# Layer normalisation and router as one block, ranking by the eight largest values, statistics and first expert weights moved ahead

## The reference

```python
x = x + s * g                       # end of layer 0; s is the mixer, g the gate
xn = _layernorm(x, axis=-1)         # (x - mean) / sqrt(var + 1e-5)
s = _L1_attn_ref(xn, ...)
g = _silu(_L1_ffn_ref(xn, ...))     # begins with the router, below
x = x + s * g

router_logits = x @ gate_w.T                            # 16 experts
routing_probs = jax.nn.softmax(router_logits, axis=-1)
topk_w, topk_idx = jax.lax.top_k(routing_probs, K)      # K = 4; of equal values the first wins
topk_w = topk_w / topk_w.sum(axis=-1, keepdims=True)
combine = (jax.nn.one_hot(topk_idx, E) * topk_w[..., None]).sum(1)
shared = _silu_mul(x @ shared_gate_up.T, SI) @ shared_down.T
shared = shared * jax.nn.sigmoid(x @ shared_gate_vec.T)
# then sum over experts of (silu-gated x @ w_gu) @ w_d * combine
```

## Time and profile before

| | |
|---|---|
| median of 3 runs | 2531.27 us (2529.53 to 2531.35) |
| the profiled execution | 2531.68 us |
| its span in the profile | 2530.0 us |
| busy in the span | PE 89%, DVE 73%, ACT 57%, POOL 51% |
| end of the mixer to the first expert matmul | 1518.78 to 1597.53, 78.75 us |

### The profile page before, as it was taken

The page is one execution under the profiler, slowest core; times in us unless marked ns, Lnnn a source line. Parts: engine busy times, 40 slices in busy tenths (PEclk is TensorE's granted clock), DMA queues, the critical chain, the costliest instruction groups (busy, mean ns, idle before and its releaser), DMA issues. The chain is left out here.

```text
span 2530.0 us, 45593 instructions
## 1 busy us (share of the span) xinstructions
PE 2259.8 (89%) x16164; PEld 1793.2 (71%) x16164; DVE 1836.3 (73%) x3256; ACT 1435.5 (57%) x2461; POOL 1289.7 (51%) x1275
## 2 busy tenths in 40 slices
PE   4996999999999999999999972799999995799992
PEld 2785788888888888888888862688888884444432
DVE  5875777777777777777777746677777776777755
ACT  1333778877878787877878851122222224266661
POOL 3451676777767777676876770354554540000000
PEclk9997999999999999999999995899999998799996
DMA  2002112112121121211211220100000002122214
GB/s 90 1 22 111 44 53 74 53 45 90 45 80 47 45 91 45 82 45 53 82 53 57 75 67 1 36 28 21 28 21 28 27 8 96 59 76 81 76 60 137
DMA packets 93441, 141.19 MB, mean 56 GB/s; under 512 B 23713, under 2 KB 62977, under 8 KB 91969
## 3 DMA queue, kind: packets, MB, share of 16 engines
q1 hardware_dynamic: 91200, 133.96, 16.1%
q10 hardware_dynamic: 2048, 4.72, 0.6%
HBM read 118.12 MB, written 20.32 MB: 55 GB/s over the span
## 5 line engine op out<-in xcount | busy, mean ns | idle before, releaser
L1081 DVE SCALAR_TENSOR_TENSOR mix_cv<-mix_pp,mix_cw,mix_cv 128x384 f32<-128x384 f32 (+4 forms) x864 | 490.8, 571 | 215.0 <-ACT mix_cv L999 194.2
L1220 POOL TENSOR_TENSOR ffn_hl<-ffn_h,ffn_hh 128x512 fp32r<-128x512 f32 x112 | 144.9, 1293 | 250.8 <-ACT ffn_hh L1278 250.8
L1024 ACT ACTIVATE mix_lm<-mix_pd 128x512 f32<-128x512 f32 x256 | 153.3, 599 | 205.1 <-PE mix_pd L915 203.1
L851 POOL TENSOR_TENSOR mix_ce<-mix_ce,mix_cv 128x1024 f32<-128x1024 f32 x112 | 266.8, 2382 | 0.0
L75 PE MATMUL mix_pp<-l0in_XH,mix_w_lo 128*128 128x384 f32 (+2 forms) x576 | 243.6, 423 | 22.9 <-DVE mix_w_lo L1069 16.2
L981 PE MATMUL mix_px<-mix_wo,mix_z 128*128 128x256 f32 x1024 | 256.4, 394 | 0.0
L1707 DVE TENSOR_REDUCE att_tops<-att_psc 128x1 f32<-128x512 f32 (+3 forms) x384 | 189.9, 550 | 55.5 <-PE att_psc L1655 32.2
L857 POOL TENSOR_TENSOR mix_zt<-mix_zsq 128x256 f32<-128x256 f32 x128 | 94.2, 736 | 243.0 <-ACT mix_zsq L1032 243.0
L1731 ACT ACTIVATE att_pr<-att_pst 128x1024 f32<-128x1024 f32 (+7 forms) x256 | 156.5, 657 | 103.5 <-PE att_pst L1672 73.5
L1278 ACT ACTIVATE ffn_hh<-ffn_h 128x512 fp32r<-128x512 f32 x112 | 71.1, 635 | 249.0 <-DVE ffn_h L1301 249.0
L981 PEld LDWEIGHTS mix_px<-mix_wo,mix_z 128*128 128x128 f32 x1024 | 186.8, 192 | 20.6
(11 more groups left out here) (332 smaller groups left out, 6873.2 us busy)
## 6 DMA issues: line engine op xcount, KB each, us to landing
mix_ce<-ecs SPq DMA_DIRECT2D x112, 512.0 KB, 3.7
mix_w_raw<-in_w_in SPq DMA_DIRECT2D x8, 1280.0 KB, 5.6
a_part<-att_sums SPq DMA_DIRECT2D x32, 256.0 KB, 5.1
ffn_raw<-in_wgu SPq DMA_DIRECT2D x56, 128.0 KB, 2.2
mix_ll<-cs SPq DMA_DIRECT2D x384, 4.0 KB
mix_wo<-in_w_out SPq DMA_DIRECT2D x8, 512.0 KB, 6.6
ffn_draw<-in_wd SPq DMA_DIRECT2D x28, 128.0 KB, 2.1
q<-qkv_part SPq DMA_DIRECT2D x24, 128.0 KB, 1.9
```

The costliest lines, as they stand in the source:

```text
L851: pool.tensor_tensor(ce[o][:, :, :], ce[o][:, :, :], cv[:, CT_C, cols_of(c)].unsqueeze(1).to_broadcast([P, GH, Q]), ALU.mult).then_inc(ce_ ...
L1024: act.activation(lm[o][:, 4 * i:4 * i + 4, :].rearrange("p h l -> p (h l)"), pd[:, :], ACT.Exp).then_inc(l_done, 1)
L1081: last = dve.scalar_tensor_tensor(out, of, cw[:, g, ct, 3 - d:4 - d], out, ALU.mult, ALU.add)
```

## The change

`layernorm` and `router` become one block, `norm_route`. What it does otherwise:

- The mixer takes bn_stats of each finished row tile at the end of the slot after it (L1022 of the new file), on DVE, behind a wait for `joined`; there is one slot more.
- POOL's pow is made in four parts of four tiles. DVE normalises the even tiles, ACT the odd ones (Identity with scale and shift). Rings are three deep, a unit is two tiles, and PE's router matmuls of a unit follow its turning at once, on 32 padded columns instead of 128; turned logits of all 16 tiles go into one PSUM bank and are copied once.
- The ranking takes the eight largest of each 16 values (MAX), compares with the fourth of them, and settles ties by a running count made with four shifted additions.
- ACT makes Tanh ahead of Exp. ACT makes high parts of the first two tiles of expert weights, POOL low parts, and POOL clears the sum; SP loads these weights at the block's start (`GluWeights`). One half of the last copy to `CW3` moves to ACT.

The diff, cut to its core (the removed `layernorm` and the removed parts of `router` are told above):

```diff
@@ mixer
-        SLOTS = range(-5, NC + 2)
+        SLOTS = range(-5, NC + 3)
...
+                    if LAST <= c - 3 < NC:
+                        i = c - 3 - LAST
+                        dve.wait_ge(joined, i + 1)
+                        dve.bn_stats(stat[:, i, :], ACC[:, i, :])
@@ glu
-                load(0, 0)
-                load(0, 1)
...
-                cut_tile(0, 0)
-                cut_tile(0, 1)
...
-                dve.memset(OUT[:, :, :], 0.0).then_inc(zeroed, 1)
-                dve.wait_ge(zeroed, 1)
@@ norm_route
+                sp.dma_start(w[:, :, 0:NE], w_route).then_inc(w_in, 16)
+                for a in range(2):
+                    weights.load(sp, 0, a, wgu, wd, sel)
...
+                for i in range(4):
+                    t = slice(i * NT // 4, (i + 1) * NT // 4)
+                    pool.tensor_tensor(rstd[:, t], var[:, t], half[:, t], ALU.pow).then_inc(powered, 1)
...
+                pool.wait_ge(logits, 1)
+                for a in range(2):
+                    pool.wait_ge(hi_cut, 3 * a + 3)
+                    pool.tensor_tensor(weights.wl[a][:, :, :, :], weights.raw[a][:, :, :, :],
+                                       weights.wh[a][:, :, :, :].bitcast(F32), ALU.subtract).then_inc(weights.cut, 1)
+                    pool.tensor_tensor(weights.dl[a][:, :], weights.draw[a][:, :], weights.dh[a][:, :].bitcast(F32),
+                                       ALU.subtract).then_inc(weights.split[a], 1)
+                pool.memset(OUT[:, :, :], 0.0).then_inc(cleared, 1)
...
+                for n in range(RING):
+                    turn(n)
+                pe.wait_ge(w_split, 2)
+                for n in range(NU):
+                    project(n)
+                    if n + RING < NU:
+                        turn(n + RING)
+                    if n >= 2 and n % 2 == 0:
+                        turn_logits(n // 2 - 1)
+                turn_logits(NU // 2 - 1)
...
+                act.wait_ge(logits, 1)
+                act.activation(cw[:, :, E:NE], lg[:, :, E:NE], ACT.Tanh, scale=0.5).then_inc(tanhed, 1)
+                act.wait_ge(routed, 2)
+                act.activation(cw[:, :, 0:E], cw[:, :, 0:E], ACT.Exp).then_inc(exped, 1)
+                for a in range(2):
+                    act.wait_ge(weights.w_in[a], 64)
+                    act.activation(weights.wh[a][:, :, :, :], weights.raw[a][:, :, :, :], ACT.Copy).then_inc(hi_cut, 1)
...
+                shift_of(0)
+                normalise(0)
+                normalise(1)
+                shift_of(1)
+                normalise(2)
...
+                for n in range(NU):
+                    low(n)
+                    if n + RING < NU:
+                        normalise(n + RING)
...
+                for t in range(NT):
+                    last = dve.max(top[:, t, :], cw[:, t, 0:E])
+                then(last)
+                least = top[:, :, TOPK - 1:TOPK].to_broadcast([P, NT, E])
...
+                for j, d in enumerate((1, 2, 4, 8)):
+                    to = 1 + j % 2
+                    then(dve.tensor_tensor(tie[to][:, :, PAD:], tie[of][:, :, PAD:], tie[of][:, :, PAD - d:PAD + E - d], ALU.add))
+                    of = to
```

More of the change, by code:

```diff
@@ L1344, in _ @@
[L1344 to L1347 removed]
+                pool.memset(half[:, :], -0.5).then_inc(powered, 1)
+                pool.memset(w[:, :, :], 0.0).then_inc(w_zero, 1)
+                pool.wait_ge(powered, 1)
+                pool.wait_ge(stats, 7)
@@ L1366, in _, with turn @@
-                pe.wait_ge(v, 25)
+                def turn(n):
+                    pe.wait_ge(even, n + 1)
+                    pe.wait_ge(odd, n + 1)
+                    if n >= RING:
+                        pe.wait_ge(lo_done, n - RING + 1)
+                    for j in range(2):
+                        for k in range(KD):
+                            last = pe.transpose(xt[n % RING][:, k * 256 + j * P:k * 256 + (j + 1) * P],
+                                                xn[(2 * n + j) % (2 * RING)][:, k * P:(k + 1) * P], ident[:, :])
+                    last.then_inc(turned, 1)
@@ L1380, in _, with normalise, keep_logits @@
-                act.activation(cw[:, :, E:NE], lg[:, :, E:NE], ACT.Tanh, scale=0.5).then_inc(a, 1)
+                def normalise(n):
+                    t = 2 * n + 1
+                    act.activation(xn[t % (2 * RING)][:, :], X[:, t, :], ACT.Identity, bias=shift[:, t:t + 1],
+                                   scale=rstd[:, t:t + 1]).then_inc(odd, 1)
+                def keep_logits(b):
+                    act.wait_ge(lg_mm, 2 * b + 2)
+                    act.activation(lg_t[:, b * TB:(b + 1) * TB], pl_[b % 2][0:W, :], ACT.Copy).then_inc(lg_kept, 1)
@@ new lines, in _ @@
+                for n in range(RING):
+                    act.wait_ge(shifted, (2 * n + 1) // 4 + 1)
+                    normalise(n)
+                for n in range(NU):
+                    act.wait_ge(turned, n + 1)
+                    act.activation(both(n)[0], turned_of(n), ACT.Copy).then_inc(hi_done, 1)
+                    if n + RING < NU:
+                        act.wait_ge(shifted, (2 * (n + RING) + 1) // 4 + 1)
+                        normalise(n + RING)
+                    if n >= 2 and n % 2 == 0:
+                        keep_logits(n // 2 - 1)
@@ L1412, in _ @@
-                then(dve.tensor_tensor(above[:, :, :, :], above[:, :, :, :], same[:, :, :, :], ALU.add))
-                then(dve.tensor_reduce(rank[:, :, :], above[:, :, :, :], AX.X, ALU.add))
-                then(dve.tensor_scalar(rank[:, :, :], rank[:, :, :], TOPK - 0.5, None, ALU.is_lt))
-                then(dve.tensor_tensor(e, e, rank[:, :, :], ALU.mult))
+                dve.wait_ge(exped, 1)
+                for t in range(NT):
+                    last = dve.max(top[:, t, :], cw[:, t, 0:E])
@@ L1416, in _ @@
+                then(dve.tensor_tensor(order[:, :, :], tie[of][:, :, PAD:], above[:, :].unsqueeze(2).to_broadcast([P, NT, E]), ALU.add))
+                then(dve.scalar_tensor_tensor(keep[:, :, :], order[:, :, :], TOPK + 0.5, tie[0][:, :, PAD:], ALU.is_lt, ALU.mult))
+                then(dve.tensor_tensor(keep[:, :, :], keep[:, :, :], over[:, :, :], ALU.add))
+                then(dve.tensor_tensor(e, e, keep[:, :, :], ALU.mult))
                 then(dve.tensor_reduce(tot[:, :], e, AX.X, ALU.add))
```

302 lines of the change are left out of this document (125 added, 177 removed).

## The result

The changed kernel takes **2488.07 us** (median of 4 runs, 2486.38 to 2495.33) against 2530.4 for the kernel before beside it: a ratio of 0.9841, interval 0.9829 to 0.9853, 42.3 us less. The forecast was 2494 and 36.9 us less, the range 2487 to 2503. A second set of runs gave 0.985 (0.9835 to 0.9865), 38.8 us less.

The account below looks back on a forecast made before the run. The prediction took a 78.75 us chain of waits between the mixer's last row and the first expert matmul as the bound. Gains 4.9 + 11.5 + 13.0 + 7.5 = 36.9 us gave 2494 us, range 2487 to 2503.

Parts of the forecast that it names:

- What bounds: From the mixer's last row to the first expert matmul, 78.75 us hardly overlap; time saved there is saved from the end.
- Statistics: At the mixer's end: bn_stats leave the dip and hide in DVE's idle time within mixer slots; gain 4.9 us.
- The rival of 5.3 us lost: In the mixer's last 16 slots: DVE sets the pace, statistics are not hidden, 5.3 us are back, 2499; chance 0.05.
- Small operations to logits: From the first small operation to whole logits: 21.1 us instead of 32.6; gain 11.5.
- the middle value: Start of the first projection: 7.5 us, between 6.3 and 8.7 if DVE's first steps each wait for a POOL pow.
- The rival in which PE stays slow: In the router's units: PE keeps its low clock, six units at 2.3 instead of 1.3, +6.0 us, 2500; chance 0.15.
- Ranking: From logits to combine weights: MAX and ten small operations replace five long passes, 17.8 us instead of 30.82; gain 13.0.
- The wait on POOL: In the ranking: POOL's subtractions for the weights hold DVE's two-input operations, 0 to 4.1 us, taken as 2.6.
- The rival in which it holds them: In the ranking: POOL's memset holds DVE's operations too, +3.4 us, 2498; chance 0.12.
- Weights: Between combine weights and first expert matmul: loads and splitting are covered, one hand-over of 1.0 us stays of 8.52; gain 7.5.
- the low end of the range: Whole time 2487: earlier projection, no port wait, cheaper MAX and small operations, earlier clock and shorter hand-over, 6.8 us together.

Follow-up runs that it names:

- e_stats_back: The changed kernel with the 16 bn_stats taken out of the mixer and put at the new block's start: 2494.11 us, ratio to before 0.9864.
- e_pairs_back: The changed kernel with the ranking by pairwise comparison, as in the kernel before, in place of MAX: 2507.14 us, ratio to before 0.9914.
- e_split_back: The changed kernel with the first expert weights loaded and split in the experts' block again, on SP and POOL: 2496.05 us, ratio to before 0.9871.
- e_same: The changed kernel with no edit, run again for its time and a second profile: 2489.93 us, ratio to before 0.985.
- e_warm: The changed kernel with 22 unread PE transposes added, 12 ahead of the first unit and 10 ahead of the projections: 2487.72 us, ratio to before 0.9819.

## Why the prediction was right, step by step

**What bounds** was right: the stretch is one of serial hand-overs, and what was taken from it was taken from the end. Of the time of e_stats_back, e_pairs_back and e_split_back against e_same (4.2, 17.2 and 6.1 us), the pieces account for 5.9, 16.9 and 5.9; the 1.7 between 4.2 and 5.9 is no more than the whole times of one kernel spread.

**Statistics**: forecast 4.9, measured 4.95. That they are hidden in the mixer holds over the sixteen rows, 135.97 us with and without them (e_stats_back). The rival of 5.3 us lost falls.

**Small operations to logits**: forecast 11.5, measured 12.1. The first projection came at 7.06 (forecast 7.5, between 6.3 and 8.7), but the reason for the middle value was wrong. POOL's pows held nothing: two normalisations beside them took 0.73, as alone. (The 4.76 of those rows spans two POOL instructions of 2.34, L328 and an L327 behind it; each normalisation waited for one.) What cost 0.9 was a cast that waits for a memset and had been overlooked. That 7.06 lies near 7.5 is luck. PE's low clock lasted 3.2 us against 4.0, and the first two units took 3.72. The six units behind them took 8.12 (1534.46 to 1542.58) against 7.8, but the forecast had the wrong engine for it. ACT was to set 1.3 per unit with PE at 1.1; in the trace PE works without a break up to the last unit, and ACT waits for it (0.25, 1.22 and 1.70 us ahead of its later copies of logits). PE's matmuls of 256 columns stand 0.117 apart instead of 0.10, and turning the logits of two units, 0.37, was counted once at the end and not between the units. That the sum came out near is luck again; that the time was PE's is shown by e_warm, where all that a faster PE saved reached the logits. The rival in which PE stays slow falls: 1.00 from 1534.4 on.

**Ranking**: forecast 13.0, measured 14.1. A MAX costs 0.083 (1.32 / 16), below the lower bound of 0.10; 0.6 from there. The wait on POOL was 2.1, forecast 2.6. The Trainium skill, "SBUF — State Buffer", has it in "SBUF: two separate sides" (and not in the section that the prediction names) that a DVE operation of two inputs in SBUF and a POOL operation that reads SBUF exclude each other. This agrees with 2.1 gone in e_split_back and with 1.30 and 4.42 grown to 4.48 and 5.37 in e_pairs_back. By that rule the memset would be free beside two-input operations, and it was: 0.42 each at 1552.96 and 1553.41. The rival in which it holds them falls. It did hold a normalisation, which has one input, for 3.09 in e_split_back, but not the reduction of e_pairs_back, 4.42.

**Weights**: forecast 7.5, measured 8.2: the hand-over at the block's end is 0.30, below the 0.48 that was taken as the lower bound. SP's loads, ACT's copies and POOL's work were all covered.

Together 39.4 against 36.9, four terms each a little too careful. The terms so explain 2.5 of the 5.4 us by which the whole was better than forecast, and 2488.07 stands only 1 us above the low end of the range. The remaining 2.9 of the 42.3 us lies outside of the stretch. One profile of the changed kernel gives back 3.0 by the mixer's last row, the other gains 1.9 there, and from the first expert matmul to the end of the span it is 932.5 us before (2530.0 - 1597.53), 932.4 and 930.9 in the two. The clock in the mixer's end is shown to go with some 3 us between two executions; how much of the 2.9 is it, and how much the spread of the runs of before (2525.35 to 2531.27 beside e_same), stays open.

## What to carry to other kernels

Where a stage is a chain of hand-overs, cost it by its ends in the timeline and not by busy time: each term here came out within 1.1 us from rows of a kernel that had none of the new operations, though the largest error inside a term, which engine sets the pace of the units, did not show in its sum. Look at what stands beside each operation of DVE and POOL, and put POOL's reading instructions away from DVE's two-input ones, and its memsets away from casts and normalisations. A table load belongs in front of a wait, so the function that needs it must be the first behind the wait.

## What was not expected of the hardware

- A memset on POOL, which reads nothing, held a DVE cast of 0.22 us for 1.60, and a normalisation of 0.41 for 3.09. Four pows on POOL (3.95 us) held no normalisation of the same form (0.73 for two).
- PE's clock rose 3.2 us into the projections after a stand of 1.16 us ahead of them, earlier (within 1.9 us) after one of 0.24, and over 5 us in where the statistics stood ahead of them (e_stats_back, 0.50 until 1536.40). 22 transposes of PE ahead of them gave 1.00 at once.
- 16 MAX of 16 values each take 1.32 us.
